# Second layer of a two-layer graph network: the one-hot comparison reads its constant row from PSUM, and the sums share two PSUM banks in pairs

## The reference

```python
ld = node_feats @ we_dst
ls = node_feats @ we_src
logit = ld[dst] + ls[src] + be
logit = jnp.where(logit >= 0, logit, NEG_SLOPE * logit)
m = jax.ops.segment_max(logit, dst, num_segments=N)
ev = jnp.exp(logit - m[dst])
denom = jax.ops.segment_sum(ev, dst, num_segments=N)
a = ev / denom[dst]
hv = node_feats @ w_proj + b_proj
msg = hv[src] * a[:, None]
c = jax.ops.segment_sum(msg, dst, num_segments=N)
context = jax.nn.elu(c)
```

## Time and profile before

| | us |
|---|---|
| median of 3 runs | 4636.18 (4626.39 to 4641.06) |
| span of the profiled execution | 4634.7 |
| PE busy | 3431.6 (74%) |
| POOL busy | 3277.4 (71%) |
| DVE busy | 2243.8 (48%) |
| ACT busy | 2123.4 (46%) |
| gathers of the second layer (L510) | 1626.4 in 1612 |
| comparisons of the second layer (L1112) | 234.6 in 124 |

### The profile page before, as it was taken

How to read it: one execution, slowest core, us unless ns; L and a number is a source line. 1 busy time by engine, 2 the same in 40 slices (tenths; PEclk the granted TensorE clock), 3 DMA queues, 4 the chain that set the end, 5 groups by cost and what they waited for, 6 DMA issues and landing times.

```text
span 4634.7 us, 95782 instructions
## 1 busy us (share of the span) xinstructions
PE 3431.6 (74%) x19691; PEld 2458.2 (53%) x19691; DVE 2243.8 (48%) x5106; ACT 2123.4 (46%) x3882; POOL 3277.4 (71%) x3396
## 2 busy tenths in 40 slices
PE   4798888888888888888577777666677766666656
PEld 3676676767766767666244444343344433334332
DVE  2465555555555555555634444444344444444436
ACT  2454444444444444444354444454454444445434
POOL 3777777777777777777377777777777777777740
PEclk8899999999999999999767667778667778878877
DMA  5655545455454554544132222232222232222210
GB/s 123 176 167 158 151 141 162 144 158 147 142 163 141 155 154 141 163 143 136 49 82 73 78 75 73 73 81 74 73 80 73 74 80 73 74 76 78 74 42 28
DMA packets 409307, 503.71 MB, mean 109 GB/s; under 512 B 101159, under 2 KB 330081, under 8 KB 409118
## 3 DMA queue, kind: packets, MB, share of 16 engines
q1 hardware_dynamic: 301598, 284.83, 19.7%
q0 software_dynamic: 104832, 216.49, 19.0%
q10 hardware_dynamic: 2690, 0.73, 0.1%
HBM read 486.41 MB, written 15.26 MB: 108 GB/s over the span
## 4 chain that ended last, share of the span: by engine, by line
POOL 50%; issue 24%; PE 14%; DMA 5%; DVE 3%; DVEq 1%; SPq 1%; POOLq 1%; ACT 1%; ACTq 0%
POOL G L510 32%; POOL G L474 18%; DMA G<-q_tab,idx 3%; PE bank L770 3%; PE bank L771 3%; PE bank L792 2%; PE bank L777 2%; PE bank L783 1%; DMA G<-x_tab,idx 1%; SPq L284 1%; DVE accT L1007 1%; POOLq L196 0%; SPq L308 0%; PE bank L739 0%; POOL idx L452 0%
## 5 line engine op out<-in xcount | busy, mean ns | idle before, releaser
L510 POOL DMA_INDIRECT G<-x_tab,idx x1612 | 1626.4, 1009 | 535.7 <-issue 500.4
L474 POOL DMA_INDIRECT G<-q_tab,idx x1612 | 1570.4, 974 | 532.4 <-issue 469.4
L1121 DVE SCALAR_TENSOR_TENSOR Z<-Z,evr,bank 128x128 f32 x1612 | 560.7, 348 | 750.8 <-PE bank L871 609.7
L871 PE MATMUL bank<-Z 128*128 128x128 f32 x3224 | 865.7, 370 | 51.6 <-DVE Z L1121 49.9
L770 PE MATMUL bank<-ident,G 128*128 128x128 f32 x3224 | 675.3, 293 | 296.4 <-DMA G<-q_tab,idx 246.6
L1007 DVE TENSOR_TENSOR accT<-accT,bank 128x128 f32 x1612 | 452.2, 281 | 910.8 <-PE bank L792 686.2
L658 ACT ACTIVATE Z<-G,evr 128x128 f32<-128x128 f32 x1612 | 597.0, 396 | 431.8 <-PE bank L871 411.6
L871 PEld LDWEIGHTS bank<-Z 128*128 128x128 f32 x3224 | 567.8, 228 | 401.2 <-issue 260.6
L836 PE MATMUL bank<-Z 128*26 128x128 f32 x3224 | 719.6, 320 | 3.7 <-ACT Z L628 3.7
L770 PEld LDWEIGHTS bank<-ident,G 128*128 128x128 f32 x3224 | 520.5, 203 | 328.9 <-issue 327.4
L771 PE MATMUL bank<-Z 128*128 128x128 f32 x3224 | 654.8, 287 | 0.0
(11 more groups left out here) (153 smaller groups left out, 2640.5 us busy)
## 6 DMA issues: line engine op xcount, KB each, us to landing
Z<-p_tab SPq DMA_DIRECT2D x1612, 64.0 KB
Z<-meta SPq DMA_DIRECT2D x62, 896.0 KB
Z<-meta SPq DMA_DIRECT2D x62, 832.0 KB
Z<-meta SPq DMA_DIRECT2D x62, 768.0 KB
G<-q_tab,idx POOLq DMA_INDIRECT x1612
G<-x_tab,idx POOLq DMA_INDIRECT x1612
Z<-ld_d SPq DMA_DIRECT2D x1612, 0.5 KB
x_tab<-X SPq DMA_DIRECT2D x13, 264.0 KB, 2.1
```

The source lines that it names most:

```text
L474: pool.indirect_dma_start(G[:, j, 0:F], None, q_tab[:, :], bass.IndirectOffsetOnAxis(ap=idx[:, j:j + 1], axis=0)).then_inc(landed[g], 16)
L510: pool.indirect_dma_start(G[:, u, :], None, x1_tab[:, :], bass.IndirectOffsetOnAxis(ap=idx[:, u:u + 1], axis=0)).then_inc(rows_landed[s], 16)
L871: nc.tensor.matmul(bank[u][:, 0:128], Gs[u], EQ[j // HC][:, j % HC, :], start=True, stop=True).then_inc(t_mm, 1)
L1121: v.scalar_tensor_tensor(out=win, in0=win, scalar=evr[:, s, 1, j:j + 1], in1=bank[(s * SC + j) % 4][:, 0:128], op0=ALU.mult, op1=ALU.add). ...
```

## The change

VectorE's comparison takes its first operand, the row 0 to 127, from PSUM and no longer from SBUF. The row is put into bank 3 once, ahead of the layer, by a product of a row of ones with iota_n. Bank 3 is free for it because the products of the sums now use banks 0 and 1 alone: two tiles in a row (a pair) lie side by side in one bank, and the pairs take the two banks in turn. TensorE begins a pair when both sums of the pair before last are done, and VectorE begins a pair's sums when both of its products are done.

```diff
@@ -158,6 +158,11 @@
+        iota_p = bank[3][:, 0:128]
+
+        def sum_bank(s, j):
+            u = s * HC + j // 2
+            return bank[u % 2][:, j % 2 * 128:(j % 2 + 1) * 128]
@@ -864,11 +869,12 @@
                 t = q * SC + j
                 u = (s * SC + j) % 4
+                if j % 2 == 0:
+                    after(pe, sum_ok, t - 2)
                 pe.wait_ge(gs_ok, t + 1)
                 if j % HC == 0:
                     pe.wait_ge(eq_ok, 2 * q + j // HC + 1)
-                after(pe, sum_ok, t - 3)
-                nc.tensor.matmul(bank[u][:, 0:128], Gs[u], EQ[j // HC][:, j % HC, :], start=True, stop=True).then_inc(t_mm, 1)
+                nc.tensor.matmul(sum_bank(s, j), Gs[u], EQ[j // HC][:, j % HC, :], start=True, stop=True).then_inc(t_mm, 1)
@@ -883,6 +889,8 @@
+            pe.wait_ge(x1t_ok, STEPS)
+            nc.tensor.matmul(iota_p, ones[0:1, :], iota_n[0:1, :], start=True, stop=True).then_inc(iota_ok, 1)
             tr_windows(0, 0)
@@ -1109,16 +1117,17 @@
                 after(dve, t_mm, (q - 1) * SC + (c + 1) * HC)
-                v.tensor_tensor(EQ[c], iota_n[:, :].unsqueeze(1).broadcast_to([128, HC, 128]),
+                v.tensor_tensor(EQ[c], iota_p.unsqueeze(1).broadcast_to([128, HC, 128]),
                                 relT[:, ds(q * SC + c * HC, HC)].unsqueeze(2).broadcast_to([128, HC, 128]), ALU.is_equal).then_inc(eq_ok, 1)
@@
                 win = cacc[:, ds(at[j % LD], 128)]
-                dve.wait_ge(t_mm, t + 1)
+                if j % 2 == 0:
+                    dve.wait_ge(t_mm, t + 2)
                 after(dve, sum_ok, t)
-                v.scalar_tensor_tensor(out=win, in0=win, scalar=evr[:, s, 1, j:j + 1], in1=bank[(s * SC + j) % 4][:, 0:128],
+                v.scalar_tensor_tensor(out=win, in0=win, scalar=evr[:, s, 1, j:j + 1], in1=sum_bank(s, j),
                                        op0=ALU.mult, op1=ALU.add).then_inc(sum_ok, 1)
@@ -1135,6 +1144,7 @@
             dve.wait_ge(cleared, 2)
+            dve.wait_ge(iota_ok, 1)
             second(0)
```

More of the change, by code:

```diff
@@ L183, in build @@
             "sq2_a", "oh2_ok", "z_ld", "z_mm", "low_ok", "lg_ok", "sc_ok", "last_tr", "run_ok", "run_tr", "cr", "dif_ok", "exp_ok", "ev_tr", "ev_ok"))
-        eq_ok, gs_ok, t_mm, sum_ok = sem("eq_ok"), sem("gs_ok"), sem("t_mm"), sem("sum_ok")
+        eq_ok, gs_ok, t_mm, sum_ok, iota_ok = sem("eq_ok"), sem("gs_ok"), sem("t_mm"), sem("sum_ok"), sem("iota_ok")
         y_ok, c_mm, mm_ok, ex_ok, ctx_ok, h1_mm, h1_ok, h2_mm, h2_ok, bn_ok = (sem(n) for n in (
```

## The result

The change takes the time from 4638.62 us (4626.39 to 4647.24 over the runs of the kernel before, the later ones included) to 4588.89 us (4578.81 to 4591.26, 4 runs). The ratio is 0.9898, with a 95% interval of [0.9876, 0.9919]: about 1% faster. The direction is the forecast one, and the time lies inside the range. But the gain is about 50 us, where 95 were forecast.

What follows compares the result with a forecast made beforehand. GpSimd's gathers and their issue gaps were taken to bound the second layer. Span 4634.7 - 98 (held gathers) + 3 (ends) = 4539.7 us, median 1.5 us above: 4541 us; own range 4525 to 4555, widened to 4600.

Steps and rivals of the forecast that it cites:

- No held gathers: Second layer, GpSimd: with the comparison's row in PSUM its gathers are no longer stretched; gain 98 us, between 92 and 105.
- held all the same: Rival: the second operand, still in SBUF, keeps holding gathers at 1.57 and 1.80 us; 4639 us, no change; chance 0.12.
- The comparison's duration: VectorE's comparison, 1892 ns, takes no longer with its first operand in PSUM; change 0.
- The waits of the pairs: TensorE and VectorE, each half pass: stricter waits add about 1.9 us (0 to 3.4), hidden under TensorE's wait.
- The ends: Last half, with no gather to hide behind, plus some handovers: 3 us lost, between 1 and 7; layer start 0.
- Behind the load everything is TensorE's pace again: After VectorE's load at tile 13, pairs take TensorE's 1.5 us against about 1.0 us of VectorE's two sums.
- the cover: TensorE's 6.6 us wait for gathered rows at L843, less 1.5 us of shorter GpSimd period: 5.1 us hides added waits.
- the slow halves: 9 of 62 half passes, 38.1 to 38.7 us with no wait at L843, clock 0.50; no reason seen for more.
- hanging work: A half pass's connected softmax, weights and 26 sums: 28.2 us before, about 30.1 us after the change.
- TensorE becomes the bound, a little: Rival: more slow halves, at fraction 0.4 a mean of 34.1 us and 4584 us in all; chance 0.08.
- The slower rival: Slow halves above fraction 0.49 push the half pass past 34.97 us; at two in three 4743 us; chance 0.05.

Runs made afterwards that it cites:

- the stop filled: The change plus four products of the identity with itself into unused bank 2 ahead of tile 16, against the kernel before: 4535.79 us, ratio 0.9783.
- the first experiment: The change without its pairs: row in bank 6, four banks, tile-by-tile handover, against the kernel before: 4532.40 us, ratio 0.9783.
- its load moved: The change with VectorE loading 14 window positions ahead of tile 0 and 12 ahead of tile 14, against the kernel before: 4538.53 us, ratio 0.9793.
- the pairs alone: The change with the comparison reading its row from SBUF again, pairs kept, against the kernel before: 4665.55 us, ratio 1.0066.
- the stop ahead of tile 6: The change with the second 13 window positions loaded right behind the second comparison, not ahead of tile 13, against the kernel before: 4912.32 us, ratio 1.06.

## Why the forecast was half right

**No held gathers: right.** The forecast had 98 us (92 to 105), and the group lost 101.2. In the kernel before, the gathers begun inside a comparison stood for 98.0 of the 105 us above the median, so the middle value was also the right share. The unknown form, first operand in PSUM and second in SBUF, frees the gathers: 1118 ns at most, and 948 ns on average in the experiment with the row alone. The rival "held all the same" is out. The rule of the Trainium skill (SBUF — State Buffer, section Who interferes with whom) that a VectorE operation with at most one SBUF input leaves GpSimd alone holds for this form too; its report that a tensor_tensor did not stall a DMA does not hold for these gathers.

**The comparison's duration: right**, 1891 ns against 1892.

**The waits of the pairs: right in size.** Tile 16's product started 22.6 us behind L848's and tile 17's 23.3, where it was 21.4: 1.9 us later, the sum that the forecast gave for the whole half. The stop was to be a gap of about 3.1 us between products; it is 3.13. And with the stop filled the halves at full clock need 29.8 to 30.1 us, where the forecast had 30.1.

**The ends: right**, 2.0 us for 3.

**The step that failed** is the sentence "Behind the load everything is TensorE's pace again", and with it the cover. TensorE's pace was taken to be a constant, 0.75 us a tile, and what a longer stop does to the clock stood in the sum at nothing, without a reason. I gave the clock to the slow halves only and argued about bursts at a half's beginning. Outside its last half the kernel before has no stop over 0.92 us at that place, so its trace did not show the clock holding behind 2.3 us. The change lengthens the one stop within the densest stretch of the half, from 0.83 to 2.31 us, and behind it the clock goes to 1.2 GHz for the last eight tiles: 6.8 becomes 10.75 us. The hanging work was 34.05 us and not 30.1. The cover of 5.1 us that was to hide 1.9 had to hide 5.85. What stuck out is the half period against the one that GpSimd alone would set (33.53 us in the first experiment): (34.24 - 33.53) x 61 = 43 us. Against the forecast span of 4539.7 us the profiled execution is 37 us long: these 43, less the 5.6 ahead of the layer and the 1 by which the ends came out shorter. By the medians 45 us of the gain are missing. "If that cover were gone, each 1 us would cost 62 us" was the right price.

**The rivals.** "TensorE becomes the bound, a little" named the right engine and, at f = 0.4, a time near the measured one (4584), but by a mechanism that did not happen: there is one slow half in the change, not two in five. It is the ordinary halves that grew. The slower rival needed still more slow halves; pairing only one side's waits (4664 and 4660 us, 28 and 26 slow halves) came near its mechanism and did lose the gain.

## What to carry to other kernels

Slack on TensorE is worth what it is only as long as its clock stays: where a change adds a wait inside a dense run of products, look up the longest stop after which the clock held in the same trace (here 0.92 us); if the new one (2.3 us) is longer, give the forecast a second branch, with what follows the stop at 1.2 GHz. A shorter lead of a fast engine shows at the one place where the slow one pauses, here a register load of 3 us; keep as many buffers as that pause needs. And when two resources free each other up (a PSUM bank for a row, banks for sums), look for room inside a bank first: the row fitted into bank 6, whose upper half was free, and that version, at 4532 us (ratio 0.9783), needs no pairs and does as well as the change with its stop filled (0.9783) or its load moved (0.9793).

## What was unexpected of the hardware

- In this dense run of products, a stop of 0.64 to 0.92 us at tile 17 left TensorE's granted clock at 1.00 in 106 halves of 106 (kernel before, and row alone). It went to 0.50 by the half's end behind 30 of 33 stops of about 1.46 us, 68 of 75 of about 1.58, 21 of 23 of about 1.72, and of those of about 2.3 behind 60 of 60 in the change and 46 of 49 in the pairs alone. With four products inside the stop and 1.22 us left, it stayed in 37 of 48.
- A clock that is down may stay down: with the stop ahead of tile 6 products at 1.28 us spacing, back to back with logit products and with no idle time on TensorE, ran at 0.80 us each to the half's end. In the run with fillers it was down ahead of tile 16 in 13 halves, and back at 1.00 behind the fillers in all 13; in none of the slow halves of the kernel before (9) or of the row alone (6) did it come back before the half's end.
- The load of 13 window positions into VectorE's registers takes 1.10 us ahead of tile 0 in the first half of each pass and 2.96 in the second, and 2.95 ahead of tile 13 in both. Of 14 positions it takes 1.32 or 3.18 us, of 12 positions 2.74 or 0.85. Which of the two levels goes with which positions are read; their number moves it by only some 0.2 us each. Why is open.
